# A graph attention layer and eight experts in one kernel: the experts' first chain placed inside the last block's weighing

## The chip, the core and the metric

One core of a Trainium2 chip. The metric is the device time of one execution in microseconds; less is better. TensorE (PE) multiplies, VectorE (DVE), ScalarE (ACT) and GpSimd (POOL) work on elements, and SyncE (SP) issues all transfers on one queue. Each engine runs its own instructions in order and waits on semaphores.

## What is computed

4096 tokens with 256 features. First a graph attention layer with a mask, then a layer normalisation, a small attention-like projection, and a mixture in which each expert takes 512 fixed tokens:

```python
x = x + gnn(adj, layernorm(x), masked_x, ...)   # scores 4096 x 4096, masked, softmax, values
x = x + ffn(layernorm(x)[None], ...)[0]
# gnn: res = le/denom @ lV + ge/denom * gV + ee/denom * eV;  return maximum(res, masked_x)
# ffn, on xf = layernorm(x):
normed = (xf - mu) / sqrt(var + 1e-05) * ln_g + ln_b
x_attn = normed @ attn_w.T + attn_b + xf
h = gelu(x_attn @ fc1_w[e].T + fc1_b[e]);  y = h @ fc2_w[e].T + fc2_b[e]
out = gelu(y @ next_w.T + next_b)
```

So the input of the experts is normalised twice: once as the layer's input (xf) and once inside the layer (normed). All products are made as three products of rounded halves (`split_product`: high x high, high x low, low x high), so each operand has a high part (made by a copy on ScalarE) and a low part (a subtraction on VectorE or GpSimd).

## The kernel before, in words

Three sections (`nc.Block`) follow one another; a section starts when the one before has ended on all engines.

**Section 1** (lines 250 to 542) normalises x, makes keys and queries, folds weights, and stores the values (`v_scratch`).

**Section 2** (lines 572 to 901) is one list of steps t = 0 to 292. There are 8 blocks of 512 queries and 32 tiles of 128 keys in each (TILES = 256). Step t scores tile t (`score`, 6 matmuls of 512 columns) and weighs tile x = t - 37 (`weigh`, 6 matmuls of 512 columns into `u_ps`). So the last 37 steps only weigh. For a tile VectorE adds the mask, keeps the running maximum and subtracts it two steps before the weighing (`centre`); ScalarE makes two exponentials, `p_hi` (three buffers) and `p_all` (two); GpSimd subtracts them into `p_lo` (two buffers, `low_weight`). SyncE loads two tiles of values at a time into a ring of three (`load_values`, 512 KB). At the end of a block the sums are read out of `u_ps` (`take_first`, `take_second`), summed (`add_up`), split and stored (`high_result`, `low_result`), and the shares are made (`shares`). `SLOTS` = 38 tiles of scores are held.

**Section 3** (lines 999 to 1503) runs the experts. The chain for block n, all inside the body of expert n - 1:

- `project` (L1378): sums and masked input times two weights, four groups of 12 matmuls of 256 columns;
- `extra_values` (POOL, L1100 to L1106): per group of tokens two scaled rows, `kt_part`, and their sum `kt`;
- `combine`, `residual` (DVE): `comb`, `res`, `resm`, `x_next`, which is the layer's residual;
- `first_moments`, `reciprocal_deviation`, `first_norm`: statistics of `x_next` (`cst`, `cmv`), deviation on POOL (`cve`, `crstd`), `xf`; `first_norm` also takes the statistics of `xf`, and `second_norm` makes `xn` from them, each for two halves of the block;
- `turn_normed`, `high_attended`, `low_attended`: `xn` is transposed by TensorE and split into `nT`;
- `attend`, `attention_bias`, `attended`: the product with the attention weight, tokens on partitions, plus `xfa` = `xf` plus a bias row (POOL);
- `turn_attended`, `high_input`, `low_input`: the result is transposed and split into `xT`.

The expert itself: eight times `first_layer` (6 matmuls, `h_ps`), gelu (`hf`), its halves, and `second_layer` (6 matmuls, `y_ps`); then `last_layer` of the expert before, the last gelu and the sum (`output`). The weights of an expert are loaded raw, copied high on ScalarE (`high_weights`) and subtracted on GpSimd (`low_weights`, `e_lo`).

The order is written out by hand in `part` and `finish`; `bodies` calls them. Body -1 holds only the first block's chain. Bodies 0, 1, 6 and 7 are written out and 2 to 5 are a hardware loop (`Fori`). In front of body -1, SyncE loads the sums, the inputs, the four split weights, the bias rows and the first expert's weights.

Of the kernel before, what the change touches and what calls it, by code (L numbers as in the profile page):

```python
# [4 lines left out]
fp32 = mybir.dt.float32  # L5
# [7 lines left out]
P = 128  # L13
KD = D // P
# [18 lines left out]
SLOTS = 38  # L33
# [22 lines left out]
def gnn_moe_kernel(nc, x, mx, mxT, adj, wlqT, wlkT, wgkT, wgqT, wgv, bgv, wes, wlv, blv, wev, bev,  # L56
# [12 lines left out]
    rows_dram = scratch("rows_scratch", (2, P, D))  # L69

    ctx = ExitStack()
    with ctx:
# [40 lines left out]
        def kblocks(ap):  # L113
# [15 lines left out]
        p_hi = rings("p_hi", [P, 3, CH], fp32r)  # L129
        p_all = rings("p_all", [P, 2, CH])  # L130
        p_lo = rings("p_lo", [P, 2, CH], fp32r)
        uT_at = rings_at + 7 * SLOT
        uT = rings("uT", [P, KD, CH])
        uT_low = nc.alloc_sbuf_tensor_at("uT_low", [P, KD, CH], fp32r, offset=uT_at)
        uT_high = rings("uT_high", [P, KD, CH], fp32r)
        top_keys = rings("top_keys", [P, CH])
        top_spread = rings("top_spread", [P, TG, P])
        early_end = rings_at + 7 * SLOT + 2 * 2 * SLOT + 2 * SLOT
        q_at = early_end
# [3 lines left out]
        v_in = rings("v_in", [P, VRING, 2, 2 * D], fp32r)  # L143
# [3 lines left out]
        dotted = rings("dotted", [P, 2, D])  # L147
        extras = rings("extras", [P, 2, 2, TG])
# [5 lines left out]
        den, extra_sum, local_top = coefs[:, 3], coefs[:, 4], coefs[:, 5]  # L154

# [7 lines left out]
        attc_b = tail("attc_b", [P, D])  # L163
# [25 lines left out]
        lnb_c = a("lnb_c", [P, KD, P])  # L189
# [4 lines left out]
        a2 = region(rings_at, early_end)  # L194
# [23 lines left out]
        xtotal_ready, xbar_ready, xbar_added, xbar_fixed, lnb_ready, rows_done, attc_done, attg_ready = (  # L218
            sem(n) for n in ("xtotal_ready", "xbar_ready", "xbar_added", "xbar_fixed", "lnb_ready", "rows_done",
# [36 lines left out]
        with nc.Block() as block:  # L256
            @block.sync
            def _(sp):
# [15 lines left out]
                sp.dma_start(lnb[:, :], ln_b).then_inc(rows_loaded, 16)  # L274
                for n, w in enumerate((wlv, wev, attn_wT, next_wT)):
                    sp.dma_start(w_all[:, n], kblocks(w)).then_inc(w_loaded, 16)
# [3 lines left out]
                def group(g, pp, h=None):  # L280
# [14 lines left out]
                    if is_group(g, NG - 2):  # L295
                        sp.dma_start(wgv_in[:, :, :], kblocks(wgv)).then_inc(wg_loaded, 16)
                        for dst, row in ((gv_b, bgv), (attc_b, attn_b), (wes_b, wes)):
                            sp.dma_start(dst[:, :], row.partition_broadcast(P)).then_inc(rows_loaded, 16)
# [55 lines left out]
            def _(dve):  # L354
# [66 lines left out]
                nc.vector.tensor_tensor(attc_b[:, :], attc_ps[:, 0:D], attc_b[:, :], ALU.add).then_inc(row_ready, 1)  # L421
# [7 lines left out]
            def _(act):  # L429
# [5 lines left out]
                def group(g, pp, h=None):  # L435
# [12 lines left out]
                    if is_group(g, 0):  # L448

                        act.wait_ge(rows_loaded, 16 * 2)  # L450
                        act.wait_ge(consts_ready, 3)
                        for k in range(KD):
                            nc.scalar.activation(lnb_c[:, k], ones[:, :], ACT.Copy, scale=lnb[:, k:k + 1]).then_inc(lnb_ready, 1)
# [7 lines left out]
                    if is_group(g, 1):  # L461

                        act.wait_ge(w_loaded, 64)
                        act.wait_ge(attc_done, 1)
# [12 lines left out]
            def _(pe):  # L477
# [8 lines left out]
                def group(g, pp, h=None):  # L486
# [25 lines left out]
                    if is_group(g, 1):  # L512

                        pe.wait_ge(lnb_ready, 2)
                        pe.wait_ge(w_loaded, 64)
                        for k in range(KD):
                            last = nc.tensor.matmul(attc_ps[:, 0:D], lnb_c[:, k], w_all[:, WATT, k], start=k == 0, stop=k == KD - 1)
# [26 lines left out]
        pb = ExitStack()  # L544
        s_ps = [ps(pb, f"s_ps{i}") for i in range(3)]
        u_ps = [ps(pb, f"u_ps{k}") for k in range(KD)]
        kept_ps = ps(pb, "kept_ps")
        mb_ps = ps(pb, "mb_ps")
        mt_ps = ps(pb, "mt_ps")
# [3 lines left out]
        phi_ready, pall_ready, plo_ready, pv_done = (sem(n) for n in ("phi_ready", "pall_ready", "plo_ready", "pv_done"))  # L553
        turned, local_ready, top_ready, spread_ready, spread_done = (
# [14 lines left out]

        with nc.Block() as block:  # L570
# [43 lines left out]
            def _(pool):  # L614
# [34 lines left out]
                for t in range(STEPS):  # L649
# [4 lines left out]
                    if 0 <= y < TILES:  # L654
                        low_weight(y)
# [878 lines left out]
```

## Time and profile before

| | us |
|---|---|
| median of 3 runs | 1185.76 (1185.70 to 1187.16) |
| the profiled execution | 1187.55 |
| its span, first to last instruction | 1185.7 |
| PE, DVE, POOL, ACT busy in the span | 1065.4, 883.9, 837.5, 528.7 |
| last scores end, last weighing begins | 758, 816.2 |
| first expert layer begins | 875.4 |

The profile gives for each engine its busy time and, by stages, how it is spread. "Busy" of PE is a union of modelled matmul times, a little longer than the spacing of the matmuls. A start is counted from the beginning of the span. In rows with a bracket, `[2.16 <-DMA ...]` is the idle time before the instruction and what ended it.

### The profile page before, as it was taken

The page shows a single profiled execution, that of the slowest core. Times are in us where ns is not written, and L with a number is a line of the kernel's source. Part 1 is how long each engine was busy: PE and PEld are TensorE (multiplying, and loading weights), DVE is VectorE, ACT ScalarE, POOL GpSimd, SP SyncE. Part 2 cuts the span into 40 slices and gives each one's busy share as a digit, 9 for nine tenths or more (in the row PEclk, how much of TensorE's full clock was granted, in tenths as well). Part 3 has the DMA queues.
Part 4 walks back from the last instruction along what each step waited for, and adds up shares of the span by engine and source line. Part 5 has one row for each costly group of instructions (what it writes and reads, how often), then busy time and mean ns, then how long its engine had stood idle before and what let it go on. Part 6 is the DMA issues. An engine that isn't in the chain of part 4 may idle for free. (4 is left out here: it accounts for less than half of the span.)

```text
span 1185.7 us, 16934 instructions
## 1 busy us (share of the span) xinstructions
PE 1065.4 (90%) x5056; PEld 879.0 (74%) x5056; DVE 883.9 (75%) x1568; ACT 528.7 (45%) x901; POOL 837.5 (71%) x868
## 2 busy tenths in 40 slices
PE   5468999999999999999999999986278999899997
PEld 3356788888888888888888888775266887778776
DVE  6866998788788788788788788750357877787773
ACT  3541043444444444444444444574135555645554
POOL 4546487687677687687687677686487789787961
PEclk9888999999999999999999999998679999999999
DMA  7895234443443443443443343354645453545321
GB/s 233 297 300 199 75 107 133 143 152 130 145 152 127 147 153 124 146 157 123 145 161 121 126 163 121 124 182 145 258 128 178 134 187 123 195 133 175 129 78 54
DMA packets 101246, 180.91 MB, mean 153 GB/s; under 512 B 10033, under 2 KB 42290, under 8 KB 100658
## 3 DMA queue, kind: packets, MB, share of 16 engines
q1 hardware_dynamic: 101170, 180.00, 45.2%
q8 instruction: 35, 0.57, 0.2%
q14 instruction: 41, 0.34, 0.1%
HBM read 144.01 MB, written 27.57 MB: 145 GB/s over the span
## 5 line engine op out<-in xcount | busy, mean ns | idle before, releaser
L627 POOL TENSOR_TENSOR p_lo<-p_all,p_hi 128x512 fp32r<-128x512 f32 x256 | 334.3, 1307 | 168.1 <-PE u_ps L853 123.1
L780 ACT ACTIVATE p_hi<-scores 128x512 fp32r<-128x512 f32 x256 | 162.0, 633 | 400.8 <-DVE scores L673 391.4
L849 PE MATMUL u_ps<-p_hi,v_in 128*128 128x512 f32 x1024 | 275.6, 391 | 3.0 <-DMA v_in<-v_scratch 2.2
L683 DVE TENSOR_TENSOR scores<-s_ps,bias 128x512 f32<-128x512 f32 x256 | 175.8, 687 | 111.6 <-PE s_ps L52 109.2
L849 PEld LDWEIGHTS u_ps<-p_hi,v_in 128*128 128x128 f32 x1024 | 191.0, 188 | 42.7 <-DMA v_in<-v_scratch 2.6
L50 PE MATMUL s_ps<-q_hi,lnT_hi 128*128 128x512 f32 x512 | 201.4, 393 | 7.5 <-POOL q_lo L632 6.7
L51 PE MATMUL s_ps<-q_lo,lnT_hi 128*128 128x512 f32 x512 | 200.0, 391 | 0.0
L52 PE MATMUL s_ps<-q_hi,lnT_lo 128*128 128x512 f32 x512 | 199.9, 390 | 0.0
L620 POOL TENSOR_SCALAR bias<-adj 128x512 f32<-128x512 uint8 x256 | 163.4, 638 | 24.1 <-DVE scores L683 22.0
L673 DVE TENSOR_TENSOR scores<-scores,mb_ps 128x512 f32<-128x512 f32 x256 | 170.8, 677 | 0.8 <-PE mb_ps L870 0.8
L697 DVE TENSOR_TENSOR kept_ps<-kept_ps,scores 128x512 f32<-128x512 f32 x232 | 162.2, 699 | 8.0
L853 PE MATMUL u_ps<-p_lo,v_in 128*128 128x512 f32 x512 | 158.0, 390 | 1.2 <-POOL p_lo L627 1.2
L782 ACT ACTIVATE p_all<-scores 128x512 f32<-128x512 f32 x256 | 157.8, 616 | 1.5 <-POOL p_lo L627 1.5
L50 PEld LDWEIGHTS s_ps<-q_hi,lnT_hi 128*128 128x128 f32 x512 | 96.6, 189 | 29.2 <-POOL q_lo L632 7.1
L853 PEld LDWEIGHTS u_ps<-p_lo,v_in 128*128 128x128 f32 x512 | 96.0, 188 | 22.1 <-POOL p_lo L627 2.1
L52 PEld LDWEIGHTS s_ps<-q_hi,lnT_lo 128*128 128x128 f32 x512 | 96.5, 189 | 20.3
L51 PEld LDWEIGHTS s_ps<-q_lo,lnT_hi 128*128 128x128 f32 x512 | 96.6, 189 | 19.7
L1086 POOL TENSOR_TENSOR e_lo<-raw,e_hi 128x512 fp32r<-128x512 f32 x64 | 96.2, 1523 | 10.0 <-ACT e_hi L1288 10.0
L1204 DVE TENSOR_TENSOR h_lo<-hf,h_hi 128x512 fp32r<-128x512 f32 x64 | 62.3, 981 | 36.5 <-ACT h_hi L1288 36.3
L1321 ACT ACTIVATE hf<-h_ps,b_c 128x512 f32<-128x512 f32 x64 | 43.7, 683 | 77.0 <-PE h_ps L52 76.9
L50 PE MATMUL y_ps<-h_hi,e_hi 128*128 128x512 f32 x128 | 51.6, 403 | 4.7 <-DVE h_lo L1204 4.7
L50 PE MATMUL h_ps<-xT_hi,e_hi 128*128 128x512 f32 x128 | 52.2, 407 | 1.5 <-DVE xT_lo L1204 1.5
(187 smaller groups left out, 1726.5 us busy)
## 6 DMA issues: line engine op xcount, KB each, us to landing
v_in<-v_scratch SPq DMA_DIRECT2D x128, 512.0 KB, 3.6
adj<-in_adj SPq DMA_DIRECT2D x64, 256.0 KB, 3.6
raw<-in_wffn SPq DMA_DIRECT2D x32, 512.0 KB, 4.0
v_scratch<-vst SPq DMA_DIRECT2D x8, 1024.0 KB, 5.2
xg<-in_x SPq DMA_DIRECT2D x8, 512.0 KB, 5.7
mg_raw<-in_mxT SPq DMA_DIRECT2D x16, 256.0 KB, 3.9
q_scratch<-q_out SPq DMA_DIRECT2D x16, 256.0 KB, 4.9
q_raw<-q_scratch SPq DMA_DIRECT2D x8, 512.0 KB, 4.6
```

The lines of the kernel that those rows point to most:

```text
L50: nc.tensor.matmul(out, l_hi, r_hi, start=start and k == 0, stop=False)
L51: nc.tensor.matmul(out, l_hi, r_lo, start=False, stop=False)
L52: last = nc.tensor.matmul(out, l_lo, r_hi, start=False, stop=stop and k == n - 1)
L620: nc.gpsimd.tensor_scalar(bias[:, t % 2], adj8[:, t // 4 % 2, t % 4 * CH:(t % 4 + 1) * CH], -MASKED, MASKED, ALU.mult, ALU.add).then_inc(b ...
L627: nc.gpsimd.tensor_tensor(out=p_lo[:, y % 2], in0=p_all[:, y % 2], in1=p_hi[:, y % 3].bitcast(fp32), op=ALU.subtract).then_inc(plo_ready, 1)
L673: nc.vector.tensor_tensor(scores[:, y % SLOTS], scores[:, y % SLOTS], mb_ps[:, :], ALU.subtract).then_inc(centred, 1)
L683: nc.vector.tensor_tensor(scores[:, t % SLOTS], s_ps[t % 3][:, :], bias[:, t % 2], ALU.add).then_inc(masked, 1)
L697: nc.vector.tensor_tensor(top_keys[:, :] if k == LASTS else kept_ps[:, :], kept_ps[:, :], scores[:, t % SLOTS], ALU.max).then_inc(kept, 1)
L780: nc.scalar.activation(p_hi[:, y % 3], scores[:, y % SLOTS], ACT.Exp, scale=SCALE).then_inc(phi_ready, 1)
L782: nc.scalar.activation(p_all[:, y % 2], scores[:, y % SLOTS], ACT.Exp, scale=SCALE).then_inc(pall_ready, 1)
L849: nc.tensor.matmul(u_ps[d][:, :], v_in[:, i % VRING, x % 2, at:at + P], p_hi[:, x % 3], start=k == 0 and part == 0, stop=False)
L853: last = nc.tensor.matmul(u_ps[d][:, :], v_in[:, i % VRING, x % 2, d * P:(d + 1) * P], p_lo[:, x % 2], start=False, stop=k == LASTS)
```

## The change

**One section.** Sections 2 and 3 become one, with the banks of PSUM shared by name. The first block's chain no longer is a body of its own. It is spread over the weigh-only steps by functions `beside(i)`, where i is the step of the last block's weighing (0 to 31), one for each engine. SyncE gets `first_loads(t)` in the same loop. The buffers are laid out anew so that those of the chain lie on memory that is free by then; `SLOTS` is 37. The last block's sum is read out beside expert 0.

**Low parts of the weights of attention.** From the fifth step of the last block on each third `p_lo` is made by VectorE (`late_low`) instead of GpSimd: nine in all.

**Second normalisation.** With v the variance of x, that of the normalised x is v / (v + eps), so the deviation of both together is (v (1 + eps) + eps^2)^-0.5. GpSimd makes both deviations from the first statistics (`deviations`), and VectorE makes `xn` and `xf` both from `x_next`.

**Input attended turned.** `attend` gives the product with features on partitions (weight stationary, `nT` moving, again 12 matmuls of 256 columns). `xf` is transposed ahead of it (`turn_first`), ScalarE adds the bias column on the way out of PSUM (`keep_first`, Identity), `attended` adds both, and no transpose follows. `xfa` goes.

**Bias and scaled rows.** `kt` is made by four scaled copies on ScalarE (`scaled_rows`) and four multiply-adds on VectorE (`extra_rows`) in place of twelve operations on GpSimd. The bias column is made in section 1 by four one-column matmuls in place of a row.

**Experts.** All eight are written out, no hardware loop; `xT` is double.

```diff
-SLOTS = 38
+SLOTS = 37
+        LAST = TILES - KT
+        def is_late(y):
+            return y >= LAST + 4 and y % 3 == 2
@@ SyncE
+                def first_loads(t):
+                    if t == TILES:          # wait score_done, masked; uT_hi
+                    if t == TILES + 1:      # uT_lo, coef4
+                    if t == TILES + 3:      # load_turned(0)
+                    if t == TILES + 5:      # w_hi[WLV:WEV+1]
+                    if t == TILES + 6:      # gvc_b, bev_b
+                    if t == TILES + 7:      # w_lo[WLV:WEV+1]
+                    if t == TILES + 9:      # load_rows(0)
+                    if t == TILES + 13:     # w_hi[WATT], w_lo[WATT]
+                    if t in (TILES + 15, TILES + 17, TILES + 19, TILES + 21):
+                        load_weights(0, (t - TILES - 15) // 2)
+                    if t == TILES + 23:     # w_hi[WNEXT], w_lo[WNEXT], nextb_b
+                    if t == TILES + 25:
+                        save(0)
+                    if t == TILES + 27:
+                        load_tokens(1)
@@ GpSimd
+                def deviations(n, q):
+                    pool.wait_ge(cmv_ready, 4 * n + 2 * q + 2)
+                    nc.gpsimd.tensor_scalar(cve[:, q, 0], cmv[:, q, :, 1], EPS, 0.0, ALU.add, ALU.add).then_inc(cve_ready, 1)
+                    nc.gpsimd.tensor_scalar(cve[:, q, 1], cmv[:, q, :, 1], 1.0 + EPS, EPS * EPS, ALU.mult, ALU.add).then_inc(cve_ready, 1)
+                    pool.wait_ge(cve_ready, 4 * n + 2 * q + 2)
+                    nc.gpsimd.tensor_tensor(out=crstd[:, q], in0=cve[:, q], in1=mhalf4[:, :, :], op=ALU.pow).then_inc(crstd_ready, 1)
+                def beside(i):
+                    if i == 6:
+                        low_masked(0)
+                    if i in (12, 13):
+                        deviations(0, i - 12)
+                    if i in (25, 27, 29):
+                        low_weights(0, (i - 25) // 2)
-                        low_weight(y)
+                    if 0 <= y < TILES and not is_late(y):
+                        low_weight(y)
@@ VectorE
+                def late_low(y):
+                    dve.wait_ge(phi_ready, y + 1)
+                    dve.wait_ge(pall_ready, y + 1)
+                    wait(dve, pv_done, y - 1)
+                    nc.vector.tensor_tensor(p_lo[:, y % 2], p_all[:, y % 2], p_hi[:, y % 3].bitcast(fp32), ALU.subtract).then_inc(late_low_ready, 1)
+                def normalise(n, q):
+                    dve.wait_ge(crstd_ready, 2 * n + q + 1)
+                    for kind, out, done in ((1, xn, xn_ready), (0, xf, xf_ready)):
+                        for s in range(2):
+                            nc.vector.tensor_scalar(out[:, 2 * q + s], x1_next[:, 2 * q + s], cmv[:, q, s, 0:1], crstd[:, q, kind, s:s + 1],
+                                                    ALU.subtract, ALU.mult).then_inc(done, 1)
+                def beside(i):
+                    # 7 extra_rows; 9 combine 0, 1, residual 0; 10 combine 2, 3, moments 0;
+                    # 11 residual 1, moments 1; 12, 13 normalise; 16 low_normed 0; 18 attended 0;
+                    # 19 low_normed 1; 21 low_input 0; 22 attended 1; 24 low_input 1
@@ ScalarE
+                def scaled_rows(n):
+                    for tt in range(TG):
+                        nc.scalar.activation(kt[:, tt], gvc_b[:, :], ACT.Copy, scale=coef4[:, 1, tt:tt + 1]).then_inc(ktg_ready, 1)
+                def keep_first(n, q):
+                    for m in range(KD):
+                        nc.scalar.activation(xa[:, m, q * RUN:(q + 1) * RUN], (vp_ps, xt_ps)[q][:, m * RUN:(m + 1) * RUN], ACT.Identity,
+                                             bias=attc_c[:, m:m + 1]).then_inc(xaf_ready, 1)
+                def beside(i):
+                    # 5 high_masked; 6 scaled_rows; 15 high_normed 0; 16 keep_first 0; 18 high_normed 1;
+                    # 20 high_input 0; 21 keep_first 1; 23 high_input 1; 25, 27, 29 high_weights
+                        if e == j == 0:
+                            high_masked(1)
+                            scaled_rows(1)
+                            high_result(BLOCKS - 1)
@@ TensorE
+                def attend(n, q):
+                    for m in range(KD):
+                        ms = slice(m * P, (m + 1) * P)
+                        last = split_product(nc, ap_ps[:, m * RUN:(m + 1) * RUN], parts(w_hi, w_lo, WATT, ms),
+                                             [(nT_hi[:, k], nT_lo[:, k]) for k in range(KD)])
+                def beside(i):
+                    # 8 project 0, 1; 9 project 2, 3; 14 turn_normed 0; 15 turn_first 0;
+                    # 17 attend 0, turn_normed 1; 20 attend 1, turn_first 1
-            with eng.Fori(2, E - 2) as e:
-                body(e)
+                for e in range(E):
+                    expert(e)
```

Inside an expert the chain of the next block keeps its places, but the turning of the normalised input begins at layer 4 instead of 5, and `attend` at 5 and 6 instead of 6 and 7.

## Rows read from the trace of the kernel before

**Rows 1.** Stages: window: us, engine busy (xinstructions), clock, DMA share, GB/s

```profile
761.00:818.00 57.00, 52.49 (x231) 41.48 (x229) 22.75 (x45) 41.36 (x73) 47.39 (x37) 1.00 0.50 167
818.00:875.40 57.40, 16.27 (x96) 14.49 (x97) 21.13 (x48) 9.97 (x15) 27.28 (x36) 0.67 0.62 220
875.40:914.70 39.30, 34.77 (x182) 28.57 (x183) 29.07 (x50) 17.96 (x29) 31.52 (x37) 0.96 0.45 148
914.70:952.50 37.80, 36.11 (x210) 30.72 (x209) 29.68 (x56) 21.20 (x35) 28.71 (x30) 1.00 0.38 126
...
1031.60:1071.10 39.50, 36.40 (x209) 30.57 (x209) 30.59 (x56) 21.19 (x35) 33.17 (x36) 1.00 0.48 159
...
1110.70:1149.40 38.70, 36.01 (x208) 30.49 (x208) 29.43 (x56) 20.25 (x34) 32.96 (x36) 1.00 0.27 94
```

**Rows 2.** Waits of TensorE from 818 us on: total us, times, longest us

```profile
PE vp_ps L50 <- DMA w_lo<-wlo_scratch: 22.4, 1, 22.4
PE ap_ps L50 <- DVE nT_lo L1204: 19.7, 16, 5.3
PE xt_ps L1374 <- DVE xn L1192: 8.4, 1, 8.4
```

**Rows 3.** Timeline of TensorE in the weigh-only steps: start us, us, what

```profile
784.71 1.21 PE L849 MATMUL u_ps<-p_hi,v_in 128*128 128x512 f32 x4 [2.16 <-DMA v_in<-v_scratch]
...
809.37 1.07 PE L849 MATMUL u_ps<-p_hi,v_in 128*128 128x512 f32 x4
...
816.17 1.07 PE L849 MATMUL u_ps<-p_hi,v_in 128*128 128x512 f32 x4
```

**Rows 4.** Timeline of GpSimd and of VectorE in the same steps

```profile
786.56 29.87 POOL L627 TENSOR_TENSOR p_lo<-p_all,p_hi 128x512 fp32r<-128x512 f32 x22 [2.52 <-PE u_ps L853]
...
772.09 15.03 DVE L673 TENSOR_TENSOR scores<-scores,mb_ps 128x512 f32<-128x512 f32 x25
```

**Rows 5.** Timeline of ScalarE in the same steps

```profile
796.02 0.63 ACT L780 ACTIVATE p_hi<-scores 128x512 fp32r<-128x512 f32 x1 [0.21 <-PE u_ps L853]
796.56 0.62 ACT L782 ACTIVATE p_all<-scores 128x512 f32<-128x512 f32 x1
```

**Rows 6.** Timeline of TensorE, first expert

```profile
875.40 0.47 PE L50 MATMUL h_ps<-xT_hi,e_hi 128*128 128x512 f32 x1 [1.50 <-DVE xT_lo L1204]
...
885.47 0.28 PE L50 MATMUL vp_ps<-w_hi,uT_hi 128*128 128x256 f32 x1
...
886.89 0.28 PE L50 MATMUL ap_ps<-w_hi,uT_hi 128*128 128x256 f32 x1
```

**Rows 7.** Groups by line behind 872 us: xcount, busy us, mean ns, idle before

```profile
L1204 DVE TENSOR_TENSOR h_lo<-hf,h_hi 128x512 fp32r<-128x512 f32 x64 | 62.3, 981 | 36.5 <-ACT h_hi L1288 36.3 <-issue 0.2
...
L1106 POOL TENSOR_TENSOR kt<-kt_part 128x256 f32<-128x256 f32 x28 | 23.0, 820 | 2.3
L1082 POOL TENSOR_TENSOR crstd<-cve,mhalf 128x2 f32<-128x2 f32 x28 | 21.6, 771 | 2.3
L1113 POOL TENSOR_TENSOR xfa<-xf,atc_b 128x256 f32<-128x256 f32 x28 | 20.7, 760 | 0.0
...
L1192 DVE TENSOR_SCALAR xf<-x_next,cmv,crstd 128x256 f32<-128x256 f32 x28 | 13.6, 526 | 1.5 <-POOL crstd L1082 1.5
L1103 POOL TENSOR_SCALAR kt_part<-bev_b,coef 128x256 f32<-128x256 f32 x28 | 19.4, 692 | 0.0
...
L1179 DVE BATCH_NORM_STATS2 cst<-xf 128x6 f32<-128x256 f32 x28 | 10.5, 418 | 0.5
L1204 DVE TENSOR_TENSOR nT_lo<-xt_ps,nT_hi 128x512 fp32r<-128x512 f32 x14 | 9.5, 676 | 0.0
```

**Rows 8.** The same view of ScalarE, whole run

```profile
L466 ACT ACTIVATE w_all<-w_all,lng 128x256 f32<-128x256 f32 x2 | 0.9, 507 | 0.0
```

**Rows 9.** Transfers: all from 826 to 842 us; value loads, whole run, us to landing

```profile
DMA packets 2829, 5.18 MB, mean 324 GB/s; under 512 B 351, under 2 KB 2311, under 8 KB 2573
...
v_in<-v_scratch SPq DMA_DIRECT2D x128, 512.0 KB, 3.6
```

More of the change, by code:

```diff
@@ L570, in gnn_moe_kernel, with last_layer_bank @@
+        def last_layer_bank(e, m):
+            return h_ps[0] if e == E - 1 and m == 1 else zp_ps
         with nc.Block() as block:
@@ new lines, in low_input, with last_bias @@
+                def low_input(n, q):
+                    qs = slice(q * RUN, (q + 1) * RUN)
+                    dve.wait_ge(xthi_ready, 2 * n + q + 1)
+                    low(xT_lo[:, n % 2, :, qs], xa[:, :, qs], xT_hi[:, n % 2, :, qs], xtlo_ready)
+                def last_bias(e, m):
+                    dve.wait_ge(z_done, 2 * e + m + 1)
+                    if e == m == 0:
+                        dve.wait_ge(rows_back, 32)
+                    wait(dve, zg_ready, 2 * e + m - 1)
+                    for s in range(2):
+                        nc.vector.tensor_tensor(zt[:, m, s], last_layer_bank(e, m)[:, s * D:(s + 1) * D], nextb_b[:, :], ALU.add).then_inc(zt_ready, 1)
@@ L820, in _ @@
                         high_result(ended)
+                    beside(t - LAG - LAST)
+                nc.scalar.activation(table_in[:, :], ident[:, 0:1], ACT.Gelu)
                 take_first(BLOCKS - 1)
-                high_result(BLOCKS - 1)
+                high_weights(0, 3)
+                high_weights(0, 4)
+                act.wait_ge(b_loaded, 32)
+                for e in range(E):
+                    expert(e)
+                for m in range(2):
+                    last_gelu(E - 1, m)
             @block.tensor
@@ L1377, in project @@
+                def parts(hi, lo, index, what):
+                    return [(hi[:, index, k, what], lo[:, index, k, what]) for k in range(KD)]
                 def project(n, tt):
+                    if n == tt == 0:
+                        pe.wait_ge(masked, TILES)
+                        pe.wait_ge(w_back, 32)
                     if tt == 0:
@@ L1381, in project @@
                         pe.wait_ge(mtlo_ready, n + 1)
-                        wait(pe, xtlo_ready, 2 * n)
+                        wait(pe, xaf_ready, 4 * n - 2)
                     elif tt == 1:
@@ new lines, in expert @@
+                    for j in range(HB - 3, HB):
+                        second_layer(e, j)
+                for t in range(STEPS):
+                    n, k = divmod(t, KT)
+                    if t < TILES:
+                        score(t)
+                    if n > 0 and k == 0 and n <= BLOCKS:
+                        turn_tops(n - 1)
+                    if n > 0 and k == 2 and n <= BLOCKS:
+                        spread_tops(n - 1)
+                    if t >= LAG:
+                        weigh(t - LAG)
+                    ended = ends_block(t)
+                    if ended is not None:
+                        add_up(ended)
+                    beside(t - LAG - LAST)
@@ L1500 @@
+                for e in range(E):
+                    expert(e)
+                for m in range(2):
+                    last_layer(E - 1, m)
 def kernel(**inputs):
```

1035 lines of the change are left out of this document (513 added, 522 removed).

## The prediction

> **What bounds the kernel now.** I read the table by stages first [rows 1]. While scores and weighing alternate TensorE is never idle, and nothing of the change touches that before the last block. From 761 on there is only weighing left, and TensorE is still busy 52.5 of 57 us. Then it is busy 16.3 of 57.4 us, at a mean clock of 0.67: this is the first chain of the experts, run alone. Each expert after it takes 37.8 to 39.6 us, in which TensorE is idle 1.7 to 3.1 us. So there are two things to win: the hole of 57 us, and about 3 us in each expert. Next the waits of TensorE behind 818 [rows 2]: the hole is a wait for weights read back (22.4 us), then one for the second normalisation (8.4), and the low parts nT_lo (19.7 in 16 places, the hole and all experts together). The hole has no bound of its own; it is latency behind a section boundary. Last the weigh-only tail itself, where the moved work must fit. A step takes 1.36 us (809.37 to 816.17 is five steps), with TensorE back to back [rows 3]. GpSimd makes one p_lo per step, 22 in 29.87 us, or 1.36 each: it is as full as TensorE. VectorE is nearly free, 25 centrings in 15.0 us and then nothing for 30 us [rows 4]. ScalarE spends two exponentials on a step, started 0.54 us apart, some 1.1 us, and has 0.3 left [rows 5].
>
> **The change, part by part.** *The hole.* Weighing ends at 817.6, and the first expert layer starts at 875.4 [rows 3, 6]. After the change all of that chain lies inside the tail, and the first layer needs only the end of the tail, xT_lo and the first e_lo, both made before it. So the 57.8 us fall away, and what is added to the tail must be paid back.
>
> *TensorE's share of the chain* comes on top, since it is full. Twelve matmuls of 256 columns take 1.42 us (885.47 to 886.89) [rows 6]. The projections are four such dozens, 5.7 us; attend is two, 2.8 us; sixteen transposes take about 1.8 us as an estimate (0.11 each, like a matmul of 256 columns). Together 10.3 us.
>
> *GpSimd's share* fits. Of the last 26 p_lo nine go to VectorE (each third one, from the fifth step of the block), which frees 9 x 1.3 = 11.7 us. The masked low part (two p_lo's worth, 2.6), two deviations (1.7 each) and three e_lo (3.9) ask for 9.9. But the frees and the asks don't fall together.
>
> *Where order stalls it.* TensorE can run only about two steps ahead of what VectorE has centred, because centring and the chain now share VectorE's queue. The worst place is step 12. There VectorE centres two steps ahead and then waits in normalise for a deviation that GpSimd computes only after its own p_lo of that centring. The loop is: centre 0.6, two exponentials 1.26, p_lo 1.3, deviations 1.7 (two short additions and a power of 0.77), four normalisings of 0.53, centre 0.6, exponential 0.63 [rows 4, 5, 7], some 8.2 us plus 0.5 for hand-overs. TensorE has work for 3.6 us of that. That is a stall of 5, and the combining in front of it costs about 1 more: 6 us. The lower bound is 0 (if VectorE is ahead when it gets there), the upper 10 (if both halves do it). I take 6, since residual and moments stand right in front. ScalarE is given seven groups of copies between steps 5 and 23 and three weight copies. A 128x256 copy with a column as operand took 0.51 us [rows 8], so the twelve or so small ones and the large ones come to about 9 us, against 27 steps of 0.3 plus the 10 us that TensorE adds. I take 2 us of stall, between 0 and 5.
>
> *The loads* are moved past the value loads on SyncE's one queue. A value load of 512 KB lands 3.6 us after issue [rows 9] and is issued four steps (5.4 us) before its use: slack 1.8 us. The worst bunch is that for the second block, 2.6 MB, issued between the third-last and second-last value loads. At the 324 GB/s that the loads of the hole reached it takes 8.1 us [rows 9]. The next value load is due 2.7 us after, so it comes 5.4 us late, less the slack: a stall of 3.6 us near the fourth-last weighing, between 0 and 8. The trace has one such stall already: 2.2 us at 784.7, behind a 1 MB store [rows 3]; it stays. In all the loads of the tail are about 20 MB with the values, 61 us at that rate, just under the new length of the tail.
>
> *Sum of the tail:* 817.6 + 10.3 + 6 + 2 + 3.6 = 839.5, and the first layer starts near 839.7 instead of 875.4. That saves 35.7 us.
>
> *Expert 0* took 39.3 us. It loses its cold start (clock 0.96 over the stretch [rows 1]), about 1.7 us. It gains the last block's sum (eight tiny matmuls, 1.0). It also gains a wait: projections of the next block need the masked low part, which GpSimd makes only after two e_lo and ScalarE's copy, behind its first gelu. TensorE reaches them 3.8 us after the start and the low part is there at about 6.6: 2.8 us. Its old idle time of 4.5 shrinks to about 1.5, as in the other experts. 39.3 - 1.7 + 1.0 + 2.8 - 3.0 = 38.4, a gain of 0.9.
>
> *Experts 1 to 6.* GpSimd loses per expert four kt (0.82), eight kt_part (the four of bev 0.69 each, the others alike), four xfa (0.76) and two powers (0.77): 13.4 of its 33.2 us [rows 1, 7]. VectorE loses four bn_stats (0.42) and aggregates and gets four multiply-adds: even. But its subtractions with both inputs in SBUF should be faster beside a freer GpSimd: h_lo took 0.98 us on average, nT_lo of the same size, with its input in PSUM, 0.68 [rows 7]. ScalarE gets eight small copies, 4 us on 21 of 39: covered by its idle time, and if that cover were gone each would cost its 0.5. On TensorE the transposes and attends are the same in number. What goes is the wait for nT_lo and xn: the second normalisation no longer waits for statistics of the first, and the turned input needs no transposing behind attend. TensorE's busy time per expert (36.1 to 36.4) is the floor; I leave 0.5 us of idle. Expert 1: 37.8 to 36.8. The four in the loop: 39.55 to 36.9 each, 10.6. Expert 6: 38.7 to 36.6. Sum 13.7 us, between 2 (another wait takes their place) and 16 (no idle). Expert 7 and the end have no chain beside them and stay.
>
> *Start of the kernel:* two small copies and one broadcast less, four one-column matmuls instead of two of 256. Nothing near the path that was not idle; 0. One score slot less: mask now waits for exponentials two steps back rather than three, and in the trace these end within one step, so 0.
>
> *Total:* 35.7 + 0.9 + 13.7 = 50.3 us off 1185.7, so a span of 1135.4. The profiled execution took 1187.55 for that span, the median of the runs is 1185.76, and I forecast the median: 1135.5.
>
> **A rule of the skill against the trace.** The trace shows the slowing by contention as a mean: 0.98 against 0.68 us [rows 7]. The Trainium skill, "SBUF — State Buffer", Who interferes with whom, says that a VectorE instruction with two SBUF inputs contends with GpSimd for a shared port, and that whoever comes second is blocked until the other is done. This speaks against the late low parts, which are such instructions: moving them to VectorE would not free GpSimd as counted. By the mean of the row the nine cost 9 x 0.3 = 2.7 us, which lie beside other work.
>
> **The rivals.** *A, the tail stretches:* each of the nine late low parts waits out a p_lo of 1.3 us on GpSimd, and the wait is on the path as the look-ahead is two steps. 9 x 1.3 = 11.7, and the load stall reaches its 8: 1135.5 + 11.7 + 4.4 = 1152. For it: GpSimd and TensorE both at 1.36 a step. Against it: the time TensorE spends on projections lets the others catch up. That is also the time the page's rule above would give. *B, the experts don't shorten:* the chain inside an expert only changes owner; ScalarE and VectorE, in order, become late instead of GpSimd. 1135.5 + 12 = 1148. For it: expert 1, which lies outside the loop, still idles 1.7 us with the same work. Against it: 13 us less on the fullest helper. *C, everything fits:* no stall in the tail but the old one, experts at TensorE's floor: 1135.5 - 11.6 - 3 = 1121. *D, slower:* the look-ahead in the tail is gone altogether, so that a step becomes its whole chain: centre 0.60, two exponentials 1.26, p_lo 1.3, and hand-overs, 3.5 us instead of 1.36. Over 32 steps that is 69 us instead of the 11.6 of stalls, 1135.5 + 57 = 1193. It decides the sign from 3.3 us a step on. Against it: VectorE was 30 us ahead, and the rings of three and two stay. *E, the change doesn't do what it says:* the first expert still waits for some load or buffer at the section's end, for instance the weights, by 10 us and more: 1148 to 1160.
>
> **How the numbers follow.** The forecast (1127 to 1145) 0.60, A 0.13, B 0.12, C 0.07, D 0.03, E 0.05. The range from 1120 to 1156 takes in A, B, C and most of E, and the ends of the bounds above where two of them add up; left out are D and the rest, under 2 in 10. About 0.2%, 2.4 us, is what a measurement can tell from no change. Faster 0.96, same 0.01, slower 0.03.
>
> **What would show it.** Right: the first h_ps near 840 with full clock, weighing ending right before it; a stall of VectorE in front of xn near 800 and one of TensorE for v_in near 825; about 36.9 us from one yf to the next; GpSimd's busy time in an expert near 20. Wrong: steps of 2 us and more throughout the tail, a wait of TensorE for e_lo or weights at the first layer, or 39 us per expert with new waits for ScalarE's nT_hi or VectorE's nT_lo.

## The result, and the profile after

The changed kernel takes 1169.14 us (median of four, 1167.18 to 1170.16) against 1185.73 for the kernel before: a ratio of 0.985, 95% interval 0.9834 to 0.9866. The forecast was 1135.5, its range 1120 to 1156. The sign was right, the size was not: a gain of 16.6 us instead of 50.3. The profiled execution took 1168.52 us for a span of 1166.7.

I begin, as before, with the table by stages; it answers to [rows 1]. The first line is the tail of the last block from the last score matmul to the first expert layer, then expert 0, experts 1, 3 and 6, and last expert 7 with the end. Columns: window: us, busy us of each engine (instructions), granted clock, DMA share, GB/s.

```profile
753.30:840.20 86.90, 72.64 (x335) 55.91 (x334) 54.20 (x95) 50.79 (x93) 46.42 (x40) 0.96 0.68 235
840.20:883.60 43.40, 37.92 (x191) 32.69 (x190) 32.95 (x52) 25.86 (x47) 25.29 (x21) 0.88 0.56 183
883.60:924.90 41.30, 37.76 (x209) 32.41 (x208) 33.05 (x53) 24.31 (x44) 19.50 (x18) 0.96 0.40 131
966.20:1007.40 41.20, 37.66 (x210) 32.37 (x209) 33.36 (x53) 24.32 (x44) 19.84 (x18) 0.96 0.47 154
1089.50:1129.40 39.90, 37.15 (x209) 32.23 (x208) 32.16 (x53) 21.81 (x38) 17.05 (x17) 0.96 0.25 88
1129.40:1166.70 37.30, 29.87 (x147) 25.09 (x146) 12.99 (x23) 19.03 (x31) 6.44 (x5) 0.91 0.12 45
```

The hole of 57 us is gone and GpSimd has fallen to some 20 us in an expert, both as expected. But an expert is *longer* than before: 41.2 us where [rows 1] have 39.5. And the clock, 1.00 in those rows from expert 1 on and 0.96 in expert 0, is now 0.96 from expert 1 on and 0.88 in expert 0. The waits of TensorE from 840 on, which answer to [rows 2], name who is late:

```profile
PE s_ps L50 <- DVE nT_lo L1017: 17.8, 7, 2.7
PE u_ps L50 <- DVE h_lo L1017: 4.8, 6, 0.8
PE s_ps L50 <- issue: 2.9, 1, 2.9
PE kept_ps L50 <- DVE y_lo L1017: 2.6, 1, 2.6
```

So experts 1 to 6 each wait 2.7 us for nT_lo in front of their first `attend` (expert 0 waits 1.8). The timelines of VectorE, GpSimd and TensorE around this wait in expert 3 (start us, us, what; in brackets idle time before it and what ended it):

```profile
986.37 0.73 DVE L1065 TENSOR_SCALAR xf<-x_next,cmv,crstd 128x256 f32<-128x256 f32 x2
...
988.29 2.10 DVE L1065 TENSOR_SCALAR xn<-x_next,cmv,crstd 128x256 f32<-128x256 f32 x2
990.31 1.68 DVE L1065 TENSOR_SCALAR xf<-x_next,cmv,crstd 128x256 f32<-128x256 f32 x2
991.91 0.68 DVE L1017 TENSOR_TENSOR h_lo<-hf,h_hi 128x512 fp32r<-128x512 f32 x1
992.51 0.68 DVE L1017 TENSOR_TENSOR nT_lo<-s_ps,nT_hi 128x512 fp32r<-128x512 f32 x1
...
987.64 1.30 POOL L852 TENSOR_TENSOR e_lo<-raw,e_hi 128x512 fp32r<-128x512 f32 x1
988.89 1.34 POOL L866 TENSOR_TENSOR o<-zg,x_here 128x512 f32<-128x512 f32 x1
990.20 1.31 POOL L852 TENSOR_TENSOR e_lo<-raw,e_hi 128x512 fp32r<-128x512 f32 x1
...
993.24 0.58 PE L50 MATMUL s_ps<-nT_hi,w_hi 128*128 128x256 f32 x1 [2.66 <-DVE nT_lo L1017]
```

Two things come together. The second half of the normalising (988.29 to 991.99) stands in VectorE's queue in front of the nT_lo of the first half, whose high part ScalarE had ready at 987.8. And its four instructions take 3.7 us, while the four of the first half take 1.4 (xf: 0.73 for two): beside the slow ones GpSimd works without a pause, beside the quick ones it has only its short operations. The twelve matmuls behind the wait then start 0.21 us apart instead of 0.12. The windows of the same expert ahead of the wait, behind it, and after that show the clock (the column ahead of the DMA share):

```profile
985.00:990.50 5.50, 5.50 (x28) 4.13 (x26) 5.46 (x14) 4.53 (x9) 4.41 (x6) 1.00 0.82 256
993.20:996.60 3.40, 3.36 (x17) 3.36 (x17) 0.98 (x2) 0.00 (x0) 0.00 (x0) 0.51 0.58 199
996.60:1000.00 3.40, 3.40 (x19) 2.90 (x18) 1.34 (x3) 2.82 (x5) 1.94 (x2) 1.00 0.00 0
```

TensorE stood still for 2.66 us and ran at the lower level, 1.2 GHz, for most of the next 3.4.

Where the forecast span of 1135.4 became 1166.7, with the experts counted from one yf to the next:

| stretch | forecast | measured | difference |
|---|---|---|---|
| up to the last score matmul | 757.5 | 753.3 | -4.2 |
| tail, to the first expert layer | 82.2 | 86.9 | +4.7 |
| expert 0, to its yf | 38.4 | 43.4 | +5.0 |
| experts 1 to 6 | 221.0 | 245.8 | +24.8 |
| expert 7 and the end | 36.3 | 37.3 | +1.0 |

Experts 1 to 6 carry 24.8 of the 31.3 us, four fifths of the miss, so the experiments begin there.

### The profile page after: what moved, and what is told of

Same layout as the page of the kernel before. It is cut to its first block, busy times and chain, and to the rows that moved or that the text cites. A ratio compares the mean times of both kernels' runs of the same rounds, so it can differ in the third digit from the quotient of the medians.

```text
span 1166.7 us, 16094 instructions
## 1 busy us (share of the span) xinstructions
PE 1076.9 (92%) x5060; PEld 892.6 (77%) x5060; DVE 914.6 (78%) x1545; ACT 550.7 (47%) x963; POOL 722.5 (62%) x715
## 4 chain that ended last, share of the span: by engine, by line
PE 66%; DVE 17%; ACT 4%; issue 4%; POOL 1%; DMA 1%; SPq 0%; DVEq 0%; ACTq 0%; POOLq 0%
PE u_ps L1396 18%; PE s_ps L50 11%; PE s_ps L52 10%; PE s_ps L51 10%; PE u_ps L1403 9%; DVE h_lo L1017 3%; DVE kt L1025 2%; DVE xn L1065 2%; DVE x_next L1048 1%; DVE comb L1035 1%; DVE xf L1065 1%; DVE scores L944 1%; DVE cst L1053 1%; DVE resm L1045 1%; PE u_ps L50 1%
## 5 line engine op out<-in xcount | busy, mean ns | idle before, releaser
L828 POOL TENSOR_TENSOR p_lo<-p_all,p_hi 128x512 fp32r<-128x512 f32 x247 | 323.2, 1309 | 196.6 <-PE u_ps L1403 124.7
L852 POOL TENSOR_TENSOR e_lo<-raw,e_hi 128x512 fp32r<-128x512 f32 x64 | 90.8, 1420 | 114.6 <-ACT e_hi L1230 114.1
L1017 DVE TENSOR_TENSOR h_lo<-hf,h_hi 128x512 fp32r<-128x512 f32 x64 | 55.6, 869 | 37.4 <-ACT h_hi L1230 37.4
L50 PE MATMUL u_ps<-h_hi,e_hi 128*128 128x512 f32 x128 | 50.6, 395 | 4.8 <-DVE h_lo L1017 4.8
L52 PE MATMUL u_ps<-h_hi,e_lo 128*128 128x512 f32 x128 | 49.9, 390 | 0.0
L51 PE MATMUL u_ps<-h_lo,e_hi 128*128 128x512 f32 x128 | 49.9, 390 | 0.0
```

Source lines behind the costliest of these rows:

```text
L50: nc.tensor.matmul(out, l_hi, r_hi, start=start and k == 0, stop=False)
L51: nc.tensor.matmul(out, l_hi, r_lo, start=False, stop=False)
L52: last = nc.tensor.matmul(out, l_lo, r_hi, start=False, stop=stop and k == n - 1)
L828: nc.gpsimd.tensor_tensor(out=p_lo[:, y % 2], in0=p_all[:, y % 2], in1=p_hi[:, y % 3].bitcast(fp32), op=ALU.subtract).then_inc(plo_ready, 1)
```

## The experiments

The spans by stage that are given here come from the profiled execution of each kernel. In nine traces whose tail is that of the changed kernel it took 86.9 to 89.1 us, so differences below 2 us in a tail decide nothing. The mean clock of the tail is 0.96 in the one of 86.9 us and 0.92 to 0.94 in the eight from 88.0 on.

**Order or contention.** Contention here means that VectorE's and GpSimd's instructions lengthen each other when they run side by side. Theory T1: nT_lo is late since it is queued behind the second half of the normalising. T2: it is late since GpSimd stretches that half. Two runs each take one of them away, and a third both.

```
# x1_order, VectorE, expert(e)
     if n < E and j == 5:
         low_normed(n, 0)
+        normalise(n, 1)
...
-    if j == 3:
-        normalise(n, 1)
# x2_pool, GpSimd, behind deviations(n, 1)
+    pool.wait_ge(xf_ready, 4 * n + 4)
     low_weights(n, 0)
# x3_both: both
```

> Only VectorE's order inside an expert is changed: the second half of the normalising stands behind the first nT_lo instead of in front of it. Theory T1 (order: nT_lo is late since it is queued behind the second half of the normalising and h_lo(4)): the wait of TensorE for nT_lo in front of the first attend falls from 2.67 us to under 0.5, the attend behind it runs at full clock (0.12 us a matmul instead of 0.21), and the period of an expert falls from 41.2 to 37.5-38.5 us; 1169 - 6 x 3 = about 1150. Theory T2 (contention: GpSimd's e_lo and output stretch the four normalisings from 1.4 to 3.7 us, wherever they stand): the stretched ops now delay nT_lo of the second half or h_lo(5) instead, and the period falls by less than 1.5 us; 1160 or more.

> VectorE's order stays as in the changed kernel; GpSimd alone waits, behind its deviations, until all of an expert's normalising is done before it makes the next e_lo. T2 (contention): the normalisings of the second half fall from 0.9 us each to 0.36-0.40, the wait for nT_lo from 2.67 to some 0.5 us, the period to 38-38.5 us, 1150. T1 (order): the ops are no longer slow but nT_lo still stands behind 1.4 us of them and h_lo(4); the wait falls only to about 1-1.5 us, and attend stays at half clock if TensorE still idles long enough; period about 39.5 us, 1160.

> Both edits of the two runs before this one: nT_lo in front of the second half of the normalising, and GpSimd waiting until that is done. If order and contention act on the same 2.7 us, this is hardly better than the better of the two alone (within 2 us of it). If they add up, the period is 37 us and the time 1143.

Measured: x1_order 1142.95 us, ratio to the kernel before 0.9622 (0.9592 to 0.9651); x2_pool 1144.62, 0.9639 (0.9611 to 0.9666); x3_both 1145.14, 0.9647 (0.962 to 0.9674). From one yf to the next the experts take 37.18, 37.4 and 37.65 us instead of 41.2. The waits of TensorE from the first expert layer on in x1_order, then the line of x2_pool for nT_lo:

```profile
PE u_ps L50 <- DVE h_lo L1017: 4.8, 6, 0.8
PE s_ps L50 <- issue: 2.9, 1, 2.9
PE kept_ps L50 <- DVE y_lo L1017: 2.6, 1, 2.6
PE s_ps L1457 <- DVE xn L1065: 1.2, 2, 1.1
...
```

```profile
...
PE s_ps L50 <- DVE nT_lo L1018: 2.1, 6, 0.4
...
```

And an expert of x1_order by stage, then VectorE of x2_pool in its second half of the normalising:

```profile
957.50:994.70 37.20, 36.18 (x210) 31.03 (x209) 32.77 (x53) 24.30 (x44) 20.30 (x18) 1.00 0.51 171
```

```profile
979.08 0.72 DVE L1066 TENSOR_SCALAR xn<-x_next,cmv,crstd 128x256 f32<-128x256 f32 x2
979.72 0.73 DVE L1066 TENSOR_SCALAR xf<-x_next,cmv,crstd 128x256 f32<-128x256 f32 x2
```

In x1_order the same four instructions, now behind nT_lo, are still slowed, to 2.7 us, and TensorE does not wait for them:

```profile
980.76 0.68 DVE L1017 TENSOR_TENSOR nT_lo<-s_ps,nT_hi 128x512 fp32r<-128x512 f32 x1
981.36 2.08 DVE L1065 TENSOR_SCALAR xn<-x_next,cmv,crstd 128x256 f32<-128x256 f32 x2
983.36 0.72 DVE L1065 TENSOR_SCALAR xf<-x_next,cmv,crstd 128x256 f32<-128x256 f32 x2
```

T1 holds for the wait and for the clock: 17.8 us of waits are gone and experts 1 to 6 run at 1.00. But T2 holds too, and better than I had written: with GpSimd kept away the same four instructions take 1.4 us instead of 3.7 in the unchanged order, and the wait is 0.4. What is refuted is that they are rivals. The wait needs both: the instructions in front, and their being stretched. Either cure brings back 24 to 26 us, and both together bring nothing more; in x3_both the longest wait for h_lo doubles to 1.6 us, and the longest h_lo itself takes 2.60 us instead of 1.75. What the runs leave untried is a third cure, `attend` back in its old place one layer later.

**What the late low parts are worth.** One part of the change undone: `is_late` always false, so GpSimd makes all p_lo.

> No late low parts: all p_lo of the last block are made on GpSimd as before. What they are worth: by the count of the prediction GpSimd would then have 9 x 1.3 = 11.7 us more work in a tail in which it is as full as TensorE, so the end of weighing (840.2 in the changed kernel) moves to 848-852 and the time to some 1179. The rival, that TensorE's projections, transposes and attends (10 us) leave GpSimd the same room: the end of weighing moves by under 2 us.

Measured: 1173.91 us (1170.78 to 1177.5), ratio 0.9899 (0.9868 to 0.9931), against 0.985 for the changed kernel. GpSimd is busy 58.9 of the tail's 90.3 us instead of 46.4 of 86.9, so the work moved as counted. But the tail grows by 1 to 3 us over the nine others, not by 8 to 12 (at the same mean clock, 0.92, three of the nine take 88.9 to 89.1). By the medians the kernel is 4.8 us slower, and its profiled execution was the fastest of the four, so the tail may understate it a little. GpSimd was not as full in the tail as I took it to be: even with all p_lo it is busy 58.9 of 90.3 us. That is nearer to the rival, by which TensorE's own additional work gives it time.

**The tail's two stalls, one at a time,** each on top of x1_order (1142.95 us, tail 89.1).

```
# x1_t1: normalise(0, 0) and (0, 1) at steps 14 and 15 instead of 12 and 13,
#        and each step of the chain behind them, on three engines, two later
# x1_t2, SyncE
-    if t == TILES + 27:
+    if t == TILES + 31:
         load_tokens(1)
```

> On the kernel with the first nT_lo moved in front (1142.95 us). In the last block's tail the normalising and all steps behind it come two steps later; the deviations on GpSimd stay. If VectorE's wait of 4.2 us for the deviations at 802 is what delays TensorE there (its gaps of 0.7 + 0.7 + 1.6 + 1.25 between 797 and 806), these shrink to under 1.5 us in all and weighing ends some 3 us sooner: 1140. The rival, that the lost time lies in the total work of GpSimd and VectorE: the gaps move to a later step and the end stays within 1 us: 1143.

> On the kernel with the first nT_lo moved in front. The bunch of loads for the second block is issued behind the last value load instead of between the third-last and second-last. If that bunch is what the values wait for, the gap of 3.1 us near 830 and the half clock behind it (five steps at up to 2.7 us instead of 1.36) go: tail 89.1 to 84-86 us. But what it carries lands later: it is issued about 828 to 834 and the masked input is needed at 846; if it is then the wait in the first expert that grows (2.9 us now), up to 3 us are given back: 1138 to 1141.

Measured: x1_t1 1142.32 us (ratio 0.9614, 0.9595 to 0.9634), tail 85.9; x1_t2 1142.54 (0.9611, 0.9595 to 0.9627), tail 87.5. TensorE in the tail of x1_order at the two places, then of x1_t1, then of x1_t2:

```profile
803.70 0.66 PE L1457 MATMUL s_ps<-ident,xn 128*128 128x128 f32 x4 [1.63 <-DVE xn L1065]
805.60 1.46 PE L1395 MATMUL u_ps<-p_hi,v_in 128*128 128x512 f32 x4 [1.25 <-ACT p_hi L1202]
...
834.33 2.07 PE L1395 MATMUL u_ps<-p_hi,v_in 128*128 128x512 f32 x4 [3.21 <-DMA v_in<-v_scratch]
```

```profile
807.73 0.73 PE L1402 MATMUL u_ps<-p_lo,v_in 128*128 128x512 f32 x2 [1.90 <-POOL p_lo L828]
...
811.24 1.17 PE L1395 MATMUL u_ps<-p_hi,v_in 128*128 128x512 f32 x4 [0.53 <-ACT p_hi L1202]
...
813.72 1.20 PE L1395 MATMUL u_ps<-p_hi,v_in 128*128 128x512 f32 x4 [0.53 <-ACT p_hi L1202]
...
833.62 1.20 PE L1395 MATMUL u_ps<-p_hi,v_in 128*128 128x512 f32 x4 [2.55 <-DMA v_in<-v_scratch]
```

```profile
833.04 1.17 PE L1395 MATMUL u_ps<-p_hi,v_in 128*128 128x512 f32 x4 [0.61 <-ACT p_hi L1202]
...
839.19 1.20 PE L1395 MATMUL u_ps<-p_hi,v_in 128*128 128x512 f32 x4 [0.52 <-ACT p_hi L1202]
```

The stall behind the bunch of loads is real and has the cause I gave it: with the bunch behind the last value load it is 0.6 instead of 3.2 us. In x1_order it also cost clock, 0.50 in the 5.2 us behind it; in the changed kernel's own trace, with the same code there, it did not. The row of TensorE and the window behind it there, then the window of x1_order:

```profile
833.88 1.20 PE L1396 MATMUL u_ps<-p_hi,v_in 128*128 128x512 f32 x4 [3.07 <-ACT p_hi L1203]
833.88:840.20 6.32, 5.86 (x25) 4.54 (x26) 1.29 (x2) 3.69 (x7) 3.74 (x4) 1.00 0.05 18
```

```profile
834.30:839.50 5.20, 5.17 (x12) 4.11 (x13) 1.29 (x2) 1.20 (x3) 1.67 (x2) 0.50 0.03 12
```

(The row of the changed kernel names p_hi, which ends at the same moment; x1_t2 shows that it is the load.) But x1_t2 did not bring what was expected of it: its tail of 87.5 us lies within the spread of the nine, not at 84 to 86, and three stalls of 0.5 to 0.7 us for p_lo and p_hi stand behind the one that went. The stall at the normalising, in x1_t1, mostly moves: 2.9 us for x1_order, 1.9 + 0.5 + 0.5 for x1_t1. That is the rival's case (total work, not place), although it had the end of the weighing within 1 us. Of the 3.2 us by which the tail of x1_t1 is shorter, 1.3 lie behind the value load, at a mean clock of 0.76 instead of 0.64 (7.2 us to the first expert layer instead of 8.5). The time of both kernels can't be told from that of x1_order.

**The first expert.** Its wait of 2.9 us is in front of the second block's projections, for the masked low part (which ends at 846.86 in the changed kernel; TensorE goes on at 846.96).

```
# x1_d, on x1_order. ScalarE: high_masked(1) ahead of take_first(BLOCKS - 1)
# GpSimd:
+    low_masked(1)
     low_weights(0, 3)
     low_weights(0, 4)
-    low_masked(1)
# x1_de0 = x1_d, and on GpSimd ahead of the last low_result:
+    pool.wait_ge(kt_ready, 8)
```

> On the kernel with the first nT_lo moved in front. The masked input's high part is made on ScalarE before the copy of the weighed sums, and its low part on GpSimd before the last two e_lo. The wait of 2.9 us in front of the second block's projections goes to under 1 us, and with it the half clock behind it: first expert 40.4 to 37.5 us, time 1140. The rival: GpSimd's two e_lo then come later and the first layer waits for them instead; the first expert stays above 39.5.

> On the run with the masked low part made early (first expert 41.6 us: the wait for it was gone, but VectorE's four extra rows took 5.75 us beside GpSimd and TensorE then waited 5.3 us for what comes behind them). Now GpSimd waits until these four are done before it makes the last block's low results and the last three e_lo. If GpSimd is what stretches them, they take 1.9-2.0 us, TensorE's wait falls from 5.3 to about 1.5 us, and the first expert to 37.5-38 us: 1141. If they are slow for another reason (transfers landing, ScalarE's copies), they stay above 4 us and the first expert at 41.6.

Measured: x1_d 1145.68 us (ratio 0.9642, 0.9625 to 0.9658): the wait is gone and the first expert is *longer*, 41.6 instead of 40.4 us. x1_de0 1140.24 (0.9608, 0.9589 to 0.9626), first expert 36.2 (its profiled execution, 1137.30, is the fastest of the four). Three timelines: TensorE of x1_d; VectorE's extra rows in x1_d; the same in x1_de0.

```profile
856.79 0.58 PE L50 MATMUL s_ps<-w_hi,uT_hi 128*128 128x256 f32 x1 [5.28 <-DVE res L1038]
```

```profile
849.47 5.75 DVE L1025 SCALAR_TENSOR_TENSOR kt<-bev_b,coef,kt 128x256 f32<-128x256 f32 x4
```

```profile
847.34 1.67 DVE L1026 SCALAR_TENSOR_TENSOR kt<-bev_b,coef,kt 128x256 f32<-128x256 f32 x4
```

This is the cleanest measurement of the contention: the same four instructions take 5.75 us beside GpSimd's low parts and 1.67 with GpSimd waiting. It also shows that the wait of 2.9 us, the one thing I had forecast of this expert, was covering another: behind it stood these rows and the combining. Taking it away alone gained nothing.

**Everything together,** and in the last run the tail's extra rows one step later as well, behind GpSimd's masked low part.

> All of it together: first nT_lo in front, normalising of the tail two steps later, loads of the second block behind the last value load, masked low part earlier. If the stalls are independent and none is hidden by another: tail 83, first expert 38, 1142.95 - 3 - 3 - 2.5 = 1134 us, which is the forecast of 1135.5 with its own stalls taken out. If the late loads and the early masked copy collide (the copy now stands in front of the sums on ScalarE and waits for the load), 1138 to 1141.

> All four moves of before (1142.37 us, tail 85.4, first expert 41.1) plus GpSimd's wait for the extra rows in the first expert: 1142.37 - 3.5 = about 1139 us; 1142 if GpSimd's later work is waited for elsewhere.

> On the best kernel so far (1137.49 us, tail 84.9). In the tail VectorE makes the four extra rows one step later, when GpSimd's masked low part (780.9 to 783.5) is over. If contention stretches them there too, they take 1.7 us instead of 4.5. If they were on the path, the tail shortens by 1 to 2 us, to 83-84; if TensorE's own wait for the masked low part sets that step, the tail stays at 84.9 within 0.5.

Measured: x1_all 1142.37 us (0.9621, 0.9599 to 0.9643), best2 1137.49 (0.9585, 0.9566 to 0.9603), best3 1137.41 (0.9585, 0.9569 to 0.9601). best2 by tail, expert 0 and expert 1:

```profile
754.30:839.20 84.90, 71.16 (x335) 53.06 (x334) 56.19 (x95) 50.89 (x94) 47.11 (x40) 1.00 0.70 240
839.20:876.30 37.10, 33.93 (x191) 28.56 (x190) 28.83 (x52) 25.75 (x47) 26.75 (x21) 1.00 0.59 202
876.30:913.50 37.20, 36.17 (x210) 31.02 (x209) 32.75 (x53) 24.31 (x44) 20.24 (x18) 1.00 0.48 155
```

By the medians x1_all gained nothing over x1_order, although its tail is 3.7 us shorter in the profiled executions. Part of that is lost in its first expert, 41.1 us, for the reason of x1_d; 1134 had been expected. With GpSimd's wait it is 37.1, and none of these stages is below full clock. In best3 the tail's extra rows take 1.66 us instead of 4.48 and the tail is 85.3: slowed, but not on the path (its first expert is 1.6 us longer than that of best2 and its end 1.2 us shorter, so the time is the same). So best2 is 32 us faster than the changed kernel with no work removed from it: instructions and loads stand elsewhere in their queues, and GpSimd waits once.

**The start,** which I had put at 0 and which came out 4.4 us shorter (first score matmul at 89.4 instead of 93.8). On x1_order, the parts removed there are put back.

```
# s1_copies: ScalarE, group 0
+    act.wait_ge(rows_loaded, 16 * 3)
+    act.wait_ge(consts_ready, 3)
+    for k in range(KD):
+        nc.scalar.activation(lnb_c[:, k], ones[:, :], ACT.Copy, scale=lnb[:, k:k + 1])
# s2_load: SyncE
-    for dst, row in ((gv_b, bgv), (wes_b, wes)):
+    for dst, row in ((gv_b, bgv), (attc_b, attn_b), (wes_b, wes)):
# s3_all: both
```

> On the kernel with the first nT_lo moved in front. Put back at the start: ScalarE's two copies in the first group of tokens (0.68 us in all) and its wait for the small loads in front of them; nothing else reads what they make. If this wait and the copies are what the start had lost, the first score matmul goes from 89.9 back to some 92-94 us and the time up by 2-4 us; if not, it stays within 0.7 us.

> On the kernel with the first nT_lo moved in front. Put back at the start: the broadcast load of the attention bias onto 128 partitions, in the second-last group. If the stretch is bound by its transfers and this one holds up those behind it, the first score matmul goes from 89.9 to 92-94 us; if not, it stays within 0.7 us. If neither of the two runs moves it, the gain comes from where the buffers now lie or from the small load in their place, and stays unexplained.

> On the kernel with the first nT_lo moved in front. Both put back at the start: ScalarE's two copies with their wait, and the broadcast load of the attention bias. If these are the start's gain, the first score matmul comes at 93-94 us, as in the kernel before, and the time is 3 to 4 us above 1143; if it stays within 88.7 to 91.7, as in the other runs, the gain comes from something else, such as where the buffers lie.

Measured: first score matmul at 91.0, 91.7 and 92.6 us; times 1143.52, 1145.27 and 1146.96 (ratios 0.9638, 0.9646, 0.9655). Twelve traces with the start of the changed kernel have it between 88.7 and 91.0. So the copies alone show nothing that this spread does not, the load alone is 0.7 us outside it, and both together account for some 2 to 3 of the 4.4 us (the time of s3_all is 4.0 us above that of x1_order). The wait for q_lo in front of the first scores is 9.1 us in s3_all and 5.0 to 7.2 in all other traces, the kernel before among them (6.7). What the rest is stays open; the moved buffers were not tried.

## Why the prediction was wrong, step by step

**Experts 1 to 6: the step that failed.** "What goes is the wait for nT_lo and xn": the wait stayed, in a new place and with a new cause. I counted which engine loses what, and took TensorE's busy time as the floor. I did not lay out VectorE's queue between the normalising and `attend`, although the diff moves `attend` one layer earlier. (That this move takes the cover away is read from the queue; no run puts `attend` back.) The floor itself was right: 37.18 us in x1_order, against 36.9 forecast, and all six together 222 us against 221. Rival B had the right subject, VectorE late instead of GpSimd, but put its price at no gain. That a wait can cost more than was there before, with the clock on top (2.66 us of waiting and some 1.2 us lost to half clock, in each expert), was in none of the rivals.

**"Beside a freer GpSimd" VectorE gets faster:** by sum yes, in the place that counted no. [Rows 7] had a sign of it: xf with a mean of 526 ns, where it takes 0.40 to 0.42 with GpSimd waiting (x2_pool, x3_both). I took the mean as the price. A mean over instructions that take 0.4 us in one place and twice that or more in another is not the price of any of them; which one it is depends on what GpSimd does at that moment.

**A rule was weighed in the wrong place.** The runs show a normalising instruction, with one tensor from SBUF, at 0.38 to 0.42 us beside a waiting GpSimd and up to 1.47 beside its products of 1.3 us, and an extra row, with two, at 0.47 and at 1.48 to 1.52 in x1_d (2.59 beside mT_lo, which itself takes 2.55). The Trainium skill, "SBUF — State Buffer", Who interferes with whom, names both: besides instructions with two SBUF inputs, a `tensor_scalar` that enters a mode using both ports contends, and the loser is blocked to the other's end. The trace agrees: the slowest last about as long as the GpSimd instruction beside them. I had held the rule only against the late low parts. Eight of those nine took 0.66 to 0.69 us and one 1.73 (at 773.6), 1.0 us too much in all where I had written 2.7. Held against each VectorE instruction in the expert, it would have pointed at the 2.3 us by which the second half of the normalising is longer (3.7 against 1.4).

**The tail:** 82.2 forecast, 86.9 measured, up to 89.1 in the same code. Both stalls are where I had put them: VectorE idle for 4.22 us in front of xn at 802.64, which TensorE saw as 1.63 and 1.25 us, and the value load behind the bunch, 3.1 us against 3.6 forecast. With smaller ones, five of 0.7 to 0.8 us for p_lo among them, TensorE is idle 14.3 us of the tail. The same steps of the kernel before:

```profile
757.50:817.60 60.10, 55.76 (x246) 44.00 (x244) 25.30 (x48) 43.02 (x75) 49.21 (x39) 1.00 0.51 167
```

They have 4.3 us of idle time, so 10.0 were added, against 11.6 forecast for all stalls: the waiting is not the miss. TensorE's busy time is. It rose by 16.9 us, and the forecast has 10.3. The sum had no term for the clock, 0.96 over the tail against 1.00: as an estimate 86.9 x 0.04, or 3.5 us. It was 0.52 for 3.1 us behind the wait for v_in at 781 and 0.51 for 3.1 us behind the stall at 805. The rest of the additional busy time is not assigned. The worth of the late low parts was mis-sized: 1 to 3 us by the tail, 4.8 by the medians, not the 11.7 that GpSimd is spared.

**Expert 0:** the wait for the masked low part was 2.9 us, 2.8 forecast. What failed is the rest. TensorE's idle time is 5.5 us against 2.8 + 1.5 forecast, with a wait of 1.8 us for nT_lo behind slowed normalising. And the sum took the clock as full, but it is 0.88: as an estimate 43.4 x 0.12, or 5 us; it was 0.50 for 3 us behind the wait of 2.9. The extra rows take 4.7 us here; x1_d shows them as what comes next.

**The start and the end:** 0 became -4.2; that the removed broadcast load lay in a stretch with a DMA share near 0.9 should have made it a term. At the end, the same wait of 2.6 us for y_lo is followed by a clock of 0.50 for 2.8 us here, and by 1.00 in the kernel before.

**What held:** the hole of 57.8 us is gone whole, the first expert layer came at 840.2 where 839.7 was forecast (by two errors of opposite sign, -4.2 and +4.7), no weight or buffer was waited for (rival E), and D's loss of the look-ahead did not come.

## What to carry to other kernels

When a change moves a consumer earlier, write out the in-order queue of the producer from the last input to the result that is waited for, and price each instruction in it beside what GpSimd does then, not by its mean. Take a wait away only after asking what stands behind it: the early masked low part and the later normalising only moved their stalls, and the first paid off once the next instructions in the queue were dealt with. When two causes meet in one wait, the cheaper of them is enough: here one line moved in VectorE's order was worth 26 us.

## What the runs showed of the hardware that I had not expected

- VectorE's 128x256 instructions beside GpSimd tensor_tensor go from 0.38 to 0.42 us to as much as 1.39 (xn) and 1.47 (xf), and from 0.47 to 1.54 (kt, and 2.59 for one in the tail), while three such GpSimd instructions beside xn and xf kept their 1.30 to 1.34. In other places it was GpSimd that was slowed: three e_lo took 4.27 us in x1_d, while VectorE made its extra rows, so there both were slowed.
- A wait of TensorE of 2.66 us was followed by a granted clock of 0.51 for 3.4 us in expert 3 of the changed kernel, and by 0.50 to 0.57 in the other five of experts 1 to 6. A wait of 2.03 us at 781 was followed by 0.52 for 3.1 us. But the same place of the same code need not agree: 3.21 us were followed by 5.2 us at 0.50 in x1_order, and 3.07 us by 1.00 in the changed kernel. The 2.6 us ahead of the last layer were followed by 0.50 in the changed kernel and by 1.00 in the kernel before and in x1_de0; the end takes 11.2 us in some traces and 12.3 to 12.8 in others, mostly for this.
